# Finer setup loads, halved column maxima and new queue orders in a two-layer decoder kernel

## The chip, the cores and the metric

The kernel runs on one core of one Trainium2 chip. The metric is the device time of one execution in microseconds (us), the median of three runs. The core has a matrix engine (TensorE, PE in the profile, with its weight loads as PEld), a vector engine (VectorE, DVE), an activation engine (ScalarE, ACT), GpSimd (POOL) and a sync engine (SP), which here only issues DMA transfers. All engines run their own instruction streams in order and wait for each other by semaphores.

## The reference

Two decoder layers over 32 sequences of 128 tokens and 256 channels. Each layer is three blocks, each followed by a residual sum and a layer norm:

```
x = LN(x + windowed_attention(x))          # A: 16 heads, window of 7 keys
x = LN(x + cross_attention(x, ctx))        # B: one head, masked
x = LN(x + routed_attention_experts(x))    # X: 8 experts, top 16 tokens each
x = LN(x + decayed_attention(x))           # C: in-block decay mask
x = LN(x + memory_attention(x, ctx))       # D, E: argmax row of ctx, then 16 heads
x = LN(x + bit_ffn(x))                     # F: 256 -> 1024 -> 256

def act_quant(x):      # per token row
    scale = 127 / clip(max(abs(x)), 1e-5)
    return clip(round(x * scale), -128, 127) / scale

def bit_ffn(x):
    h = einsum(act_quant(x), weight_quant(w1))     # 1024 hidden channels
    h = silu(depthwise_conv1d(h, width 3))
    return einsum(act_quant(h), weight_quant(w2))
```

The windowed attention multiplies, for each of seven offsets, the values shifted by -3 to +3 tokens with their weights, and adds the seven products.

## The kernel before

**Tiling.** Two sequences form a group (`GB = 2`, `T = 256` tokens); there are 16 groups. A group goes through nine stations: Q (load of the transposed x, projections to queries, keys and values of the windowed attention), A (the rest of that attention), B, X, C, D, E and F. A tenth, S, is the setup, which runs once. Groups overlap: while one is in F, later ones are in A, B, X and so on.

**Order.** Each engine's instruction stream is written by `walk`, which reads a string of station letters (`ORDER["PE"]`, `ORDER["DVE"]`, `ORDER["ACT"]`, `ORDER["POOL"]`, `ORDER["SP"]`) and each time takes the next step of that station, up to its next `yield`. So an order of some 950 (PE), 1,260 (ACT) and 1,660 (DVE) letters fixes what stands behind what. A step whose semaphore is not there yet holds everything behind it on its engine.

**The start.** SP issues, in this order, the weights `wq0`, `wk0`, `wv0` (256 KB each), the transposed x of group 0 (`xT0`, 256 KB), twelve small and middle loads for the connection weights and constants, the context of group 0 for B, seven factors of products of weights, x of group 0, `xmask` and `wv0x`, the decay bits, and then in one step (line 398 to 402) `wr`, `cos_sin`, `blk`, `iota128`, the expert weights `wqkv_e` (3,072 KB) and `wo_e` (1,024 KB). Only then come the shifts of group 0 (lines 420 to 426): six of the seven windows are copied from SBUF to SBUF by two DMAs each, 252 KB a window. Behind these stand the transposed x of group 1 (line 377), seven loads for D and F (line 404; 801 KB), `raw1` (1,024 KB), x of group 1, the context of group 0 for D (line 438), and `raw2` (1,024 KB). All go through one DMA queue.

On PE, the first step of D (`D0`, key and value projection `wkv1x`) waits for the seven loads of line 404 and for the context of line 438. DVE adds up the shifted windows in thirteen steps (lines 1101 and 1105); PE then turns the sum (line 579), and only then may it project the values of the next group, whose copy by ACT lets SP issue the next shifts. `xT0` and the windows `vw` have one buffer each, so the groups' Q and A form a ring.

**The feed-forward.** The hidden channels come in four pieces of 2 x 128 (`NJ = 4`). For each piece PE multiplies, DVE scales (line 1305), ACT and DVE convolve, gate and take magnitudes, and DVE keeps the running maximum in `top_f`, 128 partitions x 512 (line 1330): columns `i * T + t`, with i the half of the piece and t the token. To get the largest value of each token over all channels, PE turns four blocks of 128 x 128 of `top_f` into `bank_f` (line 889), and DVE reduces 128 x 512 to 128 x 2 (line 1351). The last three setup steps of DVE are the reciprocals of the mean weights and the sum of `w2q` over the hidden channels (line 1039).

Of the kernel before, what the change touches and what calls it, by code (L numbers as in the profile page):

```python
# [11 lines left out]
ALU = mybir.AluOpType  # L12
# [3 lines left out]
P = 128  # L16
# [3 lines left out]
GB = 2  # L20
# [66 lines left out]
        "FEEEEFFEEFFFBBAFFAXXFXBFBFFFAXFAFXAAAAEFEAFXFAAFCCAAAAAAACCFAAFFAXAEEFFQQFFQEQFFFDDDFXXXAXXAXXXXEEXEEFXE"
        "EEEFFFBBFFBAFFABFFFFXXFAAXFFFXAAAEFXAFEAAAFAAAAXAACCEFFFEXCACFFFFEAFAAAQQFFFQDDDAAQXXXXXXXXXFEEXFFFEFEFE"
        "BBEEEAFFXFFBABXXXFFFAAFFXAAEXAFEFFAAAFCCAXFAAAFCFAAAAECEFFXAFFEAAFAQQFFFDDDQAAXXQXXXXXXXEEEXFEXEEEEFFFBF"
        "BFFFAAFFBFBXXXFFAAFFFXAXAAAAEFFCECAAAAACFAAAXFFFCAAXEEAAAFFFFQQEQQFDDDFFFAXXXXXXXAXXEEFXXEFEFFEBFBEEEFFA"  # L90
        "FAFFFBBFXXFXAAFFFXXAAAAAFFEEFCCAAAAFXCFFCAAAAXAEAEFFFFQQQQAEAADDDFXFXXFXXXFXXXAEEAXFEFEEEFFEBEBFXBFFFAAF"
        "FFBXXXFFFFFXEXEAAFFXFAAAACACAAAACFFACFAAAAAAAAEEXFFFFEDDDFQQFQFFXQXEEXXXAAXXXXFEFXEEFEFXBEBEFFFFBAAFFFXX"
        "XFBAAFFFEXXEAFXAAFFAAFAAAAACCAAAAAFFCFCEEAAXAQQQEFFFFAAXQXDDDXXXXFFXXXFFEEEFXEEEEEFFFXBBFFFFAAFXFXBXBFAA"
        "FFFFEEFXXFFAAAAAFAACXCAAAAAACACAFFFEXEAFAAFQQFFEQXXQXXXXFDDDXXXAFAFFXEEEXFEEFFFEEEFBBFFFAAFFFXXFXBBAAFFF"
        "FEEAXAAXAAFFAACCFXAAFCFFCFAEEFFFXAAAEAAAAAFFFDFDDXXAXXXXEEXXXEXFEEEEFEXFFBBFFFFBXXXBFFFFEEXXFFFFFFFCCFXF"
        "FFEECCFFFXEFXXFFXFXXDDDXXXXXXFEEFFFEEFEFEFEFECCFFFFXXFFCXFFCFFXXEEFFFFFEEFFFXDEDXDFFFFEEEFEEEEEFCCFFFFFC"
# [27 lines left out]
class Steps:

# [37 lines left out]
def build(nc, io, out):  # L163
    ctx = ExitStack()
    with ctx:
# [287 lines left out]
        def _(pe):  # L453
# [78 lines left out]
            def queries(g):  # L532
# [3 lines left out]
                if g == 0:  # L536
                    pe.wait_ge(qkv_in, 16 * 3)
# [1274 lines left out]
```

## Time and profile before

| | |
|---|---|
| time, median of 3 runs | 1081.63 us (1080.34 to 1083.15) |
| the profiled execution's own time | 1083.18 us |
| its span, first to last instruction | 1081.4 us |
| PE busy | 938.1 us (87%) |
| weight loads busy | 685.2 us (63%) |
| DVE busy | 864.5 us (80%) |
| ACT busy | 774.6 us (72%) |
| POOL busy | 165.1 us (15%) |
| moved by DMA | 59.04 MB |
| mean granted TensorE clock | 0.957 of full |

Times in the views count from the first instruction. Line numbers are those of the kernel before. In the timeline, consecutive instructions of one kind are merged into one row with their count; the bracket at its end is the idle time of the engine ahead of it and what ended it.

### The profile page before, as it was taken

What the parts mean: (1) busy time and instruction counts of PE and PEld (TensorE: products, weight loads), DVE (VectorE), ACT (ScalarE), POOL (GpSimd) and SP (SyncE); (2) the same over time, 40 slices, a digit from 0 to 9 for tenths busy, and PEclk for the clock granted to TensorE, in tenths of its full rate; (3) what the DMA queues carried; (4) which work ended last, traced back from release to release, by engine and by line L of the source; (5) the groups of instructions that cost most, each with busy time, mean ns of one, the idle gap of its engine ahead of it and who ended that gap; (6) DMA issues with size and microseconds to landing.
All of it is one profiled execution on the core that took longest, in us unless ns stands there. A gap on an engine that the chain in (4) does not pass through costs nothing.

```text
span 1081.4 us, 20184 instructions
## 1 busy us (share of the span) xinstructions
PE 938.1 (87%) x7318; PEld 685.2 (63%) x7318; DVE 864.5 (80%) x2281; ACT 774.6 (72%) x1921; POOL 165.1 (15%) x404
## 2 busy tenths in 40 slices
PE   6588798999998999999999999999999888887652
PEld 4455566767776676767676777777676666565321
DVE  5585775789888979898899989898989785866754
ACT  2166564768877878877788878787878787867653
POOL 2010210202103030302021211212020201010000
PEclk9789999999999999999999999999999999998765
DMA  9723112030120203030302011121102000000000
GB/s 326 237 75 97 38 51 78 1 108 1 42 67 28 70 21 97 11 97 11 98 1 79 30 59 49 36 73 49 59 28 71 11 2 20 2 30 1 11 11 10
DMA packets 36626, 59.04 MB, mean 55 GB/s; under 512 B 6656, under 2 KB 15872, under 8 KB 36016
## 3 DMA queue, kind: packets, MB, share of 16 engines
q1 hardware_dynamic: 36528, 57.76, 17.1%
q8 instruction: 58, 0.95, 0.4%
q14 instruction: 40, 0.33, 0.1%
HBM read 28.77 MB, written 4.19 MB: 30 GB/s over the span
## 4 chain that ended last, share of the span: by engine, by line
PE 55%; ACT 18%; DVE 17%; issue 3%; SPq 2%; DMA 2%; POOL 1%; ACTq 0%; POOLq 0%; DVEq 0%
PE bank_c L456 15%; PE bank_a L456 8%; PE banks_e L456 6%; PE bank_x L456 6%; PE bank_f L456 4%; PE bank_x L666 3%; ACT squares_out L1389 2%; SPq L426 2%; ACT area_e L1605 2%; DVE area_f L1314 2%; DVE neg_top L1254 2%; PE banks_e L835 2%; DMA area_a<-in_xT 2%; ACT area_f L1652 2%; PE bank_a L562 2%
## 5 line engine op out<-in xcount | busy, mean ns | idle before, releaser
L1314 DVE SCALAR_TENSOR_TENSOR area_f<-area_f,w_convw 128x254 f32<-128x254 f32 x256 | 111.7, 478 | 9.2 <-ACT area_f L1639 7.5
L1254 DVE TENSOR_REDUCE neg_top<-banks_e 128x8 f32<-128x1024 f32 x64 | 76.2, 1220 | 30.1 <-PE banks_e L456 29.9
L1377 ACT ACTIVATE area_bx<-bank_x 128x512 f32<-128x512 f32 (+1 forms) x144 | 70.1, 499 | 27.7 <-PE bank_x L666 11.5
L1101 DVE TENSOR_TENSOR area_a<-area_a 128x512 f32<-128x512 f32 x112 | 74.7, 683 | 10.9 <-DMA area_a<-area_a 10.3
L1639 ACT ACTIVATE area_f<-area_f,w_convb,w_convw 128x256 f32<-128x256 f32 x128 | 69.8, 596 | 15.0 <-DVE area_f L1305 14.8
L1046 DVE TENSOR_TENSOR area_a<-area_a 128x512 f32<-128x512 f32 x112 | 73.4, 683 | 5.1 <-PE bank_a L562 2.9
L1605 ACT ACTIVATE area_e<-banks_e 128x512 f32<-128x512 f32 x128 | 68.3, 601 | 8.9 <-PE banks_e L835 8.7
L1377 ACT ACTIVATE area_bx<-bank_c 128x512 f32<-128x512 f32 x64 | 34.3, 536 | 52.9 <-PE bank_c L456 39.4
L1105 DVE TENSOR_TENSOR area_a<-area_a 128x512 f32<-128x512 f32 x96 | 65.8, 685 | 0.3
L1377 ACT ACTIVATE area_a<-bank_a 128x512 f32<-128x512 f32 (+1 forms) x80 | 43.9, 549 | 30.8 <-PE bank_a L456 21.2
L456 PE MATMUL bank_x<-area_bx 128*128 128x128 f32 (+1 forms) x256 | 51.9, 336 | 5.8 <-ACT area_bx L1377 4.3
L456 PE MATMUL bank_a<-area_a,w_wq 128*128 128x256 f32 x128 | 37.1, 442 | 19.1 <-DMA area_a<-in_xT 19.1
L456 PEld LDWEIGHTS bank_x<-area_bx 128*128 128x128 f32 x256 | 40.8, 191 | 17.5 <-ACT area_bx L1377 8.5
L1305 DVE TENSOR_TENSOR area_f<-bank_f,area_f 128x512 f32<-128x512 f32 x64 | 43.8, 684 | 7.7 <-PE bank_f L456 7.7
L456 PE MATMUL bank_f<-area_f,w1q 128*128 128x256 bf16 x256 | 41.8, 290 | 9.3 <-DVE area_f L1305 7.9
L1644 ACT ACTIVATE area_f<-area_f 128x512 f32<-128x512 f32 x64 | 40.4, 632 | 13.0 <-DVE area_f L1314 12.6
L1678 POOL TENSOR_SCALAR bn_negmean_b<-bn_sums_b 128x2 f32<-128x2 f32 x16 | 4.7, 294 | 288.8 <-DVE x L918 288.8
L666 PE MATMUL bank_x<-w_wqkv_e,area_bx 128*32 128x384 f32 x512 | 47.9, 492 | 0.0
L1377 ACT ACTIVATE area_e<-banks_e 128x256 bf16<-128x256 f32 (+1 forms) x64 | 34.5, 540 | 15.6 <-PE banks_e L821 6.8
L1324 DVE SCALAR_TENSOR_TENSOR area_f<-area_f 128x512 f32<-128x512 f32 x64 | 43.8, 684 | 2.1 <-ACT area_f L1644 1.5
L456 PE MATMUL banks_e<-chosen_key,chosen_q 32*128 32x256 f32 x512 | 38.6, 417 | 7.0 <-DVE neg_top L1254 3.9
L1652 ACT ACTIVATE area_f<-area_f 128x512 f16<-128x512 f32 x64 | 37.6, 624 | 9.4 <-DVE area_f L1362 9.4
(315 smaller groups left out, 2635.3 us busy)
## 6 DMA issues: line engine op xcount, KB each, us to landing
area_a<-area_a SPq DMA_DIRECT2D x96, 224.0 KB
area_a<-in_xT SPq DMA_DIRECT2D x16, 256.0 KB, 3.0
area_bx<-in_ctxT SPq DMA_DIRECT2D x16, 256.0 KB, 3.0
x<-in_x SPq DMA_DIRECT2D x16, 256.0 KB, 3.6
area_d<-in_ctxT SPq DMA_DIRECT2D x16, 256.0 KB, 2.9
y<-x SPq DMA_DIRECT2D x16, 256.0 KB, 2.2
w_wqkv_e<-in_wqkv_e SPq DMA_DIRECT2D x1, 3072.0 KB, 11.5
area_f<-in_raw SPq DMA_DIRECT2D x2, 1024.0 KB, 11.1
```

The costliest lines, as they stand in the source:

```text
L456: last = pe.matmul(out_ap, l, r, start=i == 0 and not opened, stop=closes and i == len(pairs) - 1)
L666: last = pe.matmul(bank_x[ES * q:ES * (q + 1), 0:3 * HP], xgf[:, c, e, :], wq[:, c, e, :], start=c == 0, stop=c == DC - 1)
L1046: return dve.tensor_tensor(product_of(wi).rearrange("p (n t) -> p n t", t=P), qT0.rearrange("p c (b t) -> p (c b) t", t=P), kT0.rearrange( ...
L1101: made[wi] = own.mark(dve.tensor_tensor(v4, v4, bc(e4[:, :, wi, :], 3, DH), ALU.mult))
L1105: added = dve.tensor_tensor(vw[:, to, :], vw[:, to, :], vw[:, wi, :], ALU.add)
L1254: dve.tensor_reduce(top[:, b, r:r + 2, :, 0].rearrange("p r (par c) -> p r c par", c=DC), banks_e[:, r:r + 2, :].rearrange("p r (c par k) ...
L1305: dve.tensor_tensor(blocks(th_f[jj % 3], 2), blocks(bank_f[:, :], 2), bc(tscale_f, 1, 2), ALU.mult).then_inc(f_h, 1)
L1314: last = dve.scalar_tensor_tensor(c4[:, i, :, dst], h4[:, i, :, src], cwt3[:, 2 * jj + i, k:k + 1], c4[:, i, :, dst], ALU.mult, ALU.add)
L1377: return act.activation(dst, src, ACT.Copy)
L1605: act.activation(pT_e[:, r * 4 * P:(r + 1) * 4 * P], bank_e[r][:, :], ACT.Exp, scale=float(DH) ** -0.5).then_inc(e_exp, 1)
L1639: last = act.activation(c4[:, i], h4[:, i], ACT.Identity, bias=w["convb"][:, j:j + 1], scale=cwt3[:, j, 1:2])
L1652: act.activation(n2_f[jj], c_f[jj], ACT.Copy, bias=ROUND16).then_inc(f_round, 1)
```

## The change

Four edits.

1. **Setup loads.** `wq0` counts on the semaphore of the transposed x (`xt_in`), `wk0` and `wv0` on their own one, and PE waits for the two only ahead of its second projection. Each of the three is a step of its own; the twelve loads that followed in one step are now two steps of six.
2. **Expert weights.** `wqkv_e` and `wo_e` become steps of their own. In the new SP order they stand behind the shifts of group 0 and the transposed x of group 1.
3. **Column maxima.** DVE takes the maximum of the two halves of `top_f` (128 x 256), PE turns two blocks in place of four, and DVE reduces 128 x 256.
4. **Orders.** All five strings are new. SP's now begins `SSSQSBSASSSSQQSSSASSDAAAABQQ`: after the expert weights come the seven loads of line 404, x of group 1, `raw1`, `raw2`, the context of group 0 for D, x of groups 2 to 5, the context of group 1 for B, the shifts of group 1 and the transposed x of group 2. In DVE's, the sum over `w2q` (line 1039) comes between two window products of group 2, where before it stood amid the window sums of that group. A PE step moves by some two places on average, some by up to sixteen.

```diff
@@ SP @@
             def setup(_):
-                for name in ("wq0", "wk0", "wv0"):
-                    sp.dma_start(w[name][:, :], io[name]).then_inc(qkv_in, 16)
-                yield
+                for name, sem in (("wq0", xt_in), ("wk0", kv_in), ("wv0", kv_in)):
+                    sp.dma_start(w[name][:, :], io[name]).then_inc(sem, 16)
+                    yield
                 for dst, name in ((c1, "c1"), (b1, "b1"), (c2, "c2"), (b2, "b2"), (c3, "c3"), (b3, "b3")):
                     sp.dma_start(dst, io[name]).then_inc(early2_in, 16)
+                yield
                 for name in ("pos", "ident", "headsum", "rows", "part", "wo0"):
...
-                for name in ("cos_sin", "blk", "iota128", "wqkv_e", "wo_e"):
+                for name in ("cos_sin", "blk", "iota128"):
                     sp.dma_start(w[name][:, :], io[name]).then_inc(xw_in, 16)
                 yield
+                for name in ("wqkv_e", "wo_e"):
+                    sp.dma_start(w[name][:, :], io[name]).then_inc(xw_in, 16)
+                    yield
@@ PE @@
             def queries(g):
-                pe.wait_ge(xt_in, 16 * (g + 1))
+                pe.wait_ge(xt_in, 16 * (g + 2))
...
-                if g == 0:
-                    pe.wait_ge(qkv_in, 16 * 3)
                 take("a")
                 project(bank_a, chunked("wq0"), xT0).then_inc(a_qk_proj, 1)
                 until("a", a_qk, 2 * g + 1)
                 yield
+                if g == 0:
+                    pe.wait_ge(kv_in, 16 * 2)
...
                 for b in range(GB):
-                    for i in range(2):
-                        at = (2 * b + i) * P
-                        last = pe.transpose(bank_f[:, at:at + P], top_f[:, i * T + b * P:i * T + (b + 1) * P], I)
+                    last = pe.transpose(bank_f[:, b * P:(b + 1) * P], top_f[:, b * P:(b + 1) * P], I)
@@ DVE @@
-                    last = dve.tensor_tensor(top_f, th_f[jj % 3], top_f, ALU.max)
-                    if jj < NJ - 1:
-                        top_step[0] = own.mark(last)
-                    else:
-                        last.then_inc(f_top, 1)
+                    top_step[0] = own.mark(dve.tensor_tensor(top_f, th_f[jj % 3], top_f, ALU.max))
...
+                dve.wait_ge(own.sem, top_step[0])
+                dve.tensor_tensor(top_f[:, 0:T], top_f[:, 0:T], top_f[:, T:2 * T], ALU.max).then_inc(f_top, 1)
+                yield
                 dve.wait_ge(f_topT, g + 1)
-                m = own.mark(dve.tensor_reduce(am_f, blocks(bank_f[:, :], GB), X, ALU.max))
+                m = own.mark(dve.tensor_reduce(am_f, blocks(bank_f[:, 0:T], GB), X, ALU.max))
@@ ORDER["SP"], first letters @@
-        "SQSBSASSSQQSSADSBQQQQBAAQQBADQQDBAQQBBQDQFAQQDFADBQQFBAFQQADBDQQFBAFAQBQDFBQAQDBQQFADFQDQABDFBAQDDFDFFFF"
+        "SSSQSBSASSSSQQSSSASSDAAAABQQBQQBQQBQQDQDQBDFAQBQDFAQQBDQBQFAFDAQBQFDAQBQDFQBQADFABQQDFABQQDQBFQADFAQBDFD"
```

## Rows read from the trace of the kernel before

**Rows 1.** The page, part 1: busy us, share of the span, instructions

```profile
span 1081.4 us, 20184 instructions
PE 938.1 (87%) x7318; PEld 685.2 (63%) x7318; DVE 864.5 (80%) x2281; ACT 774.6 (72%) x1921; POOL 165.1 (15%) x404
```

**Rows 2.** Windows over long stretches: busy us by engine, PEclk, DMA share, GB/s

```profile
30.00:60.00 30.00, 17.48 (x79) 13.44 (x82) 16.90 (x45) 5.83 (x17) 1.57 (x4) 0.77 0.60 184
60.00:90.00 30.00, 23.31 (x130) 17.15 (x126) 25.78 (x71) 21.58 (x46) 3.84 (x8) 0.89 0.21 62
90.00:120.00 30.00, 22.21 (x154) 15.46 (x147) 21.50 (x44) 15.58 (x38) 3.07 (x4) 0.91 0.29 87
...
240.00:840.00 600.00, 573.42 (x4721) 424.97 (x4713) 540.83 (x1434) 486.31 (x1229) 105.52 (x245) 1.00 0.16 49
...
960.00:1081.00 121.00, 67.10 (x458) 42.36 (x456) 75.37 (x172) 69.74 (x150) 8.33 (x24) 0.74 0.03 9
```

**Rows 3.** Timeline of SP's DMA issues: start us, us, what

```profile
16.82 0.43 SPq L401 DMA_DIRECT2D w_wqkv_e<-in_wqkv_e  x1
...
18.50 8.73 SPq L426 DMA_DIRECT2D area_a<-area_a  x12
27.28 0.53 SPq L377 DMA_DIRECT2D area_a<-in_xT  x1
...
35.63 1.54 SPq L438 DMA_DIRECT2D area_d<-in_ctxT  x1
...
68.03 0.52 SPq L377 DMA_DIRECT2D area_a<-in_xT  x1
```

**Rows 4.** Timeline of DVE around the first window sums

```profile
28.33 0.39 DVE L1090 TENSOR_TENSOR area_a<-area_a 128x224 f32<-128x224 f32 x1
...
39.72 1.89 DVE L1101 TENSOR_TENSOR area_a<-area_a 128x512 f32<-128x512 f32 x3 [10.32 <-DMA area_a<-area_a]
```

**Rows 5.** Timeline of PE, 40 to 71 us

```profile
40.19 3.78 PE L456 MATMUL bank_a<-area_a,w_wq 128*128 128x256 f32 x8 [9.62 <-DMA area_a<-in_xT]
...
55.65 1.15 PE L456 MATMUL bank_c<-w_wkv1x,area_d 128*128 128x144 f32 x8
...
56.78 1.97 PE L456 MATMUL bank_a<-w_wv,area_a 128*128 128x256 f32 x8
...
59.52 1.07 PE L562 MATMUL bank_a<-area_a,w_headsum 128*32 128x256 f32 x16
61.12 0.66 PE L487 MATMUL bank_c<-w_ident,x 128*128 128x128 f32 x4 [0.53 <-ACT x L1396]
...
70.72 3.39 PE L456 MATMUL bank_a<-area_a,w_wq 128*128 128x256 f32 x8 [0.72 <-DMA area_a<-in_xT]
```

**Rows 6.** Windows of 5 us: busy us by engine, PEclk, DMA share, GB/s

```profile
15.00:20.00 5.00, 3.48 (x28) 2.36 (x28) 4.17 (x11) 2.60 (x4) 0.00 (x0) 1.00 1.11 388
...
30.00:35.00 5.00, 0.57 (x3) 0.09 (x2) 0.00 (x0) 0.00 (x0) 0.00 (x0) 0.76 1.05 250
...
60.00:65.00 5.00, 3.40 (x36) 1.89 (x28) 4.56 (x13) 3.55 (x6) 0.00 (x0) 1.00 0.52 158
```

**Rows 7.** Timeline, 112 to 120 us: the sum of w2q, and PE behind it

```profile
112.69 3.64 DVE L1039 TENSOR_REDUCE area_s<-w2q 128x256 f32<-128x2048 f16 x1
...
118.31 1.12 PE L579 MATMUL bank_a<-w_ident,area_a 128*128 128x128 f32 x4 [3.67 <-DVE area_a L1105]
```

**Rows 8.** Timeline of PE at full clock: four turns, two turns

```profile
256.53 0.60 PE L889 MATMUL bank_f<-w_ident,area_f 128*128 128x128 f32 x4
...
256.96 0.39 PE L492 MATMUL bank_c<-w_ident,area_c 128*128 128x128 f32 x2
```

**Rows 9.** Groups of instructions: lines, then a timeline row of the half size

```profile
L1351 DVE TENSOR_REDUCE area_f<-bank_f 128x2 f32<-128x512 f32 x16 | 10.9, 680 | 6.0 <-PE bank_f L889 6.0
...
95.97 0.43 DVE L1193 TENSOR_TENSOR area_bx<-area_bx 128x256 f32<-128x256 f32 x1
...
96.77 0.42 DVE L1123 TENSOR_REDUCE area_bx<-area_bx 128x2 f32<-128x256 f32 x1
```

More of the change, by code:

```diff
@@ L87 @@
[L87 to L96, printed above, removed]
@@ L97 @@
-        "FCFFFFEEFFFFFFFEEFFFDFDDFFFEFEEFFFEEEEEEFFFFFFFFEEFFFFFFFFFFFEEFFFFFFFEFFFFFFFFFFFFFFFFFFFFFFFFFFFFFFF"
+        "SSSQSQQQASSSSASSSASSSSSSSSAASAAASAASSSASSSSAAAAAAAAAAAAQQQQSSSSSSSSSSSSSSAASSSAASSSSSSSSBBSAABSSSSAAABAA"
+        "AAAAAAAAAAAAASSQXXXXXXXXXAXQQQXASAASXBBXXAABAAAXXBXAAAAAAAAAAAAAAAQQQQXAAXXXXXXXXXAXXABBBXBAAXXAAAAAAAAA"
+        "XXAAAXACCAAAAACQQQQXCAAXXXXXXXXXAXXADDDXXEXEAABEEBEEEEXXBAAAAAAAAABAXAAAAEEAAAAQQQCCQCEECXEAAFFFDDDXXXAA"
+        "XXXFXXEXFXEFFXFEEEEEEFBBFFXXBXFFBFAAFFAAAFFFXXFFAAEECCFCXFAAAAAAACAAEEFFFAAAFXFFFEAQQQQFDDDFFFAXXXXXAXXX"
@@ new lines @@
+        "XEXEXFEEEEEFEFFFFBBFFBFFXFAAXXFFBAAEFFAFAAXFXAEAXFAFFCCAAACAAAACEFFFEAQQQFFFFEXQAFAAAFFFDDDAXXXAXXXXXXEF"
+        "EXFXEEEEEFFFBAEBFFFAFBFXXXBFFFFXXAAFEFAAAXEAFAFAACCFAAFCAAAAACEAFFFAAXFFEAQQQQFFEDDDXFXXFFFAXXXXXXAEXEXE"
+        "FEFEEEEFFFBFFFBAAFFBFFFXXXFFAAFBAAAXFXAFXAEEAAAAFFCCAAAAAFCFFCFEEFFXAFQQQEAAFAQXXXXXFFFXDDDXXXAAFFEFEFXF"
+        "AFFEEEEEFEFBBFBAFFFBXXXXAAFAAAFEFXXFFEXAAAFFCCAFAAFFCAAAAAEECFFFXAFAAEAQFQQQFFFXXADDDXXXXXXXAAAEEFXEEEXE"
+        "EEFFFFBBFFXFBFBXXFAFFFAXFAAAFFXAAFFEEAFCCFXAAACAACAAAFFFEEAXAAAFFFFQQQEDDDQFAFFFXXXXXEXEAXXXEFXEXEEEFFFB"
@@ new lines @@
+        "FBFABFFAEFFFXFBXXFFAFFAXAXFAAAAFAFEEFCCAAACAAFFFAAACXAEEAAAQXFFFFQQEQFDDDXXXXXFFFAAXXEEXXFEXEEEFFFEEFXBB"
+        "FFAAFFBFXFBFXXFFFFAAXEXEFFAXFCCFAAAAACFAAACEFFEAAAAAAFAAAXFFFQQQEDDDQXFXFFFXAXXXEEXAXXEFEXEEEFFFEXBBFFFB"
+        "AFAFFXFFBXXFAAFFEAXEXAAFAAXAFFAAAAFFCCFAAAAECAEFFCAAXAFFFFEQQQAQAXXDDDXXFXXXFFFXXAAEXEXEFEEEEEFFFFBBFFFB"
+        "FXXFXBFFFEAAFFEFFXFXAAAAAAAAACCAAAAXFEFCACAFEXFFAAFFFAFQQQEXXXQXXXXDDDXFXFFFAAXXEEEFEEFEEFFEFBBFFFAAFFBF"
+        "XFXXBFFFAAFAAAEAXAAEXFFXACCFFAAAFFFACFFCFEEFAAAAXAAEAFFFFXDDDXXAXXXXXXXXEFEFFEEEEFBBEFEFXBFFXXBFFFFXXFFE"
@@ new lines @@
+        "CXBXCAXCXXBXCQDADXAXDADDDXBXABCEQXEBEEEQEXBCXBCEEXEECECXCEXCADXXDEADEQAXFFDFDDDFABBFFXFBXEBXFFBEEXFEEFCA"
+        "FBCFEFBCXQXFCXEEECEQEXCXDCEFDXFFFEDAXXEFXDFDADDFFAFQBFBXBFFFEXEBFFBXEEEFFCEAFBXACFFBQXCFXEEEECQECXCXEDXF"
+        "FFFCXEDFEDAFXXFFXDADFDDQAFBBXBFFFXEBFFBXEEFEEXFACEBFACBXFFCXQFEEXEECQECXXCCDXDEAXXDFFFFXEEDFDDDAFQFFABFF"
+        "BXBFFFEXFEEFFBEECFXAFCEBFXAFBQXCXBFEEXEECECXQXCFFFEXFDCXXEDXFEDAFFFDFADDDFQAFBFFBFXBXFFBXEBEEEEABCFEAXFC"
+        "BFFXQCXFEEEECEXDXCXCEFFFCXFEQXXDAFEDXFFFADQFDDDABFBXBEFXFFBXBFEEEEFAFEXCFFAFCBQFCXFXQBXCXCEEEEXECDCXDEFF"
@@ new lines @@
+        "FFDAXXEDFEDDDXFAFFQABFFBXBFFFBXBFFFEXFEEEEACFXEBAFCBFXFCXQCXEEXEECQEXCDECXDFFFFXDXEAFXEDFDDDFFAFBFABXBFQ"
+        "FFBXFBEFXEEEEFFACFEXFCBAFXCFBXEECEEQCXECXQDCXDFEXFDFXXFEAXDEFDDDFFFABFABFQBXFFFBXFBEFXFEEEEFAFEXACFBXQFC"
+        "BQFCEEEXECXEXCXECXCDAXXDEFFDFXFEADFQDDDFFFABFFBXBEFFFXBEBEEFXFEFAEBFXFACFBFQCXEEFCEXEXCEXCXCDXCEQXXDXFFF"
+        "DFEAEDFDDDFAFFQABFFBXBFFFBEXFFEEEXBEFFFEACXBACFBFCXFEEXCXEEXDECFFXCFFECBXDEXXEDXFAFFDFADDDFAFXBFBXFBFXBE"
+        "FFEEEEBXCEFFBFXCEFFECFXEEXCXECXFFFCEXDFCXXEDFXEDFFFFDDDDFCXCFFCFXFFCXFCEFFFEEEEXCFEDXFXCEEXEEXFEFDXFFDEX"
@@ L112 @@
+        "DEXDDDFECFFFCFCFECEFFFECEEFFCFEFFDCFEEEEFDEFDEFFDFFDDEDFEFFFFEFEEEEFFFEFFFEEFFEEFFEFEFFFFEFEFFFFFFFFFFFF"
         "FFFFFFFFFF"
```

45 lines of the change are left out of this document (16 added, 29 removed).

## The prediction

> **What bounds the kernel now.** I read the page's busy times first [rows 1]: PE has 938.1 us of work in a span of 1081.4 us, so it stands idle for 143.3 us, and DVE for 217. The average hides three different stretches, so the second view is the table of long windows [rows 2]. From 240 to 840 us PE is busy 573.42 of 600 us (96%) at full clock, DVE 540.83 (90%): there the length is PE's work plus 4% of gaps, and whatever reaches PE earlier at 240 us ends the stretch earlier by as much. From 30 to 60, 60 to 90 and 90 to 120 us PE does 17.48, 23.31 and 22.21 us of work, so 27 us are idle within 90, with the clock at 0.77, 0.89 and 0.91 of full. The last 121 us hold 67.10 us of PE work: one or two groups, a chain of latencies.
>
> So the start is where time can be had. The third view is SP's issues [rows 3] beside the waits of DVE and PE [rows 4, 5]. The shifts of group 0 are issued from 18.50 us to 27.23, the transposed x of group 1 at 27.28. DVE has its weights at 28.72 and is through its other steps at 29.40 (39.72 less 10.32 of idling), and yet adds the first window at 39.72, when the shifts have landed [rows 4]. PE waits 9.62 us for the transposed x, until 40.19 [rows 5]. What they wait for is the traffic ahead of them in the one queue: 4,096 KB of expert weights, issued at 16.82 us [rows 3]. The 5-us windows say that the transfer engines are full then: share 1.11 and 388 GB/s at 15 to 20 us, 1.05 and 250 GB/s (shifts among them) at 30 to 35 us [rows 6]. At 388 GB/s 4,096 KB (4.19 MB) take 10.8 us, which is the wait.
>
> **The change part by part.**
>
> *Weights behind the shifts.* SP reaches the shifts no sooner, since they wait for ACT's copy of the values. Without the 4.19 MB ahead they should land as those of a later group do: the transposed x issued at 68.03 lets PE start at 70.72 [rows 3, 5], 2.7 us later. From 27.28 that gives 30.0 us for both, DVE gains 39.72 - 30.0 = 9.7 us and PE 10.2. PE's projection also finds a warm clock: eight matmuls took 3.78 us after the long idle and 1.97 us later [rows 5], worth some 1.8 us. In the new order DVE adds its thirteen windows almost without setup steps between (about 0.6 us each, the three of 39.72 take 1.89), so they end near 38.5. PE turns them, and projects the values of group 1 near 42, where it ended at 58.75 before.
>
> That lead isn't kept whole. Behind the values PE has the output projection of group 0, the first head sums of group 1, and then the first step of D, and it waits for loads that now stand behind the weights: weights 4,096 KB, the seven loads 801, x 256, raw1 and raw2 2,048, context 256, together 7,457 KB or 7.64 MB. From 27.8 us at 388 GB/s that is 19.7 us, with 2.7 us until they are seen 50.2 us. Behind that step stand the second scores of A, the chain of B and all the rest, so PE idles from about 46 to 50. It did that step at 55.65 before, and then the values (1.97) and the first head sums (1.07) of group 1 [rows 5], which now lie ahead of it. So the lead behind it is 55.65 - 50.2 + 3.0 = 8.5 us. The next point is the transposed x of group 2: x of groups 2 to 5 and a context (1,280 KB, 3.4 us) also stand ahead, then the shifts (5 us at share 0.52 over 8.7 us [rows 3, 6]); it is there near 59.5. PE reaches it 70.72 - 61.12 = 9.6 us after the turning of x for B [rows 5], which starts near 52.5, so near 62: 8.7 us ahead. I take 9 us. The ends: at the 250 GB/s of the worst window the 7.64 MB take 30.6 us, D's step comes at 61.1, 5.5 us later than before, less 3.0: a loss of 2.5 us. With no hindrance the lead is the 10.2 us and the 1.8 of clock: 12 us. The window with 250 GB/s is one in which shifts moved, the loads here are from HBM, so I stay near the 388.
>
> The Trainium skill, page "DMA: Bandwidth & Descriptors", section Specifications, gives a core some 358 GB/s from HBM. By that the 7.64 MB take 21.3 us, D's step comes at 51.8, and the lead would be 1.6 us smaller; the trace goes beyond that figure with 388 GB/s in the window from 15 us.
>
> *Finer steps for wq0, wk0, wv0, and the waits.* Nothing: the transposed x is issued fourth in both orders and lands last. The context of B now stands ahead of six small loads: DVE's first setup step comes up to 1 us later (256 KB at 250 to 388 GB/s), and DVE has that slack, since it was free 0.6 us ahead of the new landing of the shifts and its products wait for ACT. 0 us, at worst -1.
>
> *The sum of w2q.* It takes 3.64 us on DVE amid the window sums of group 2, and PE behind it idles for 3.67 us and then works at half clock: four turns in 1.12 us [rows 7] where 0.60 is the full-clock time [rows 8]. In the new order it stands between the products of group 2, ahead of the second head sums. Some of it falls into DVE's own waits there, some delays the products. Between 0 and 5 us (idle, and some 1.4 of clock); I take 2.5.
>
> *Column maxima.* On PE four turns take 0.60 us and two take 0.39 [rows 8]: 0.21 us less, 16 times, 3.4 us. In the stretch in which PE is busy 96% this shortens the group's period; in the first and last groups it doesn't count as such, so 3.0 us, between 0 and 3.4. On DVE the reduction falls from 680 ns to 420, and a 128x256 maximum of 430 ns is added [rows 9]: +0.17 us a group at most, 2.7 us in all. DVE is 90% busy next to PE's 96 [rows 2], so it is covered by 59 us of DVE idle in that stretch; in the last group it is on the path: 0.43 - 0.26 - 0.21 = 0 us. Uncovered it would cost 2.7 us.
>
> The Trainium skill, page "Trainium Kernel Development and Optimization", section Performance Expectations, warns that matmul busy time is a poor measure, since matmuls are pipelined, and sends one to the weight loads; these are busy 424.97 of 600 us, 71% [rows 2]. By that PE needn't be the bound in the middle, and the 3.0 us of this term would be nothing.
>
> *The orders.* A PE step moves by some two places. What they can move is the idle time: 26.6 us in the middle stretch [rows 2], some 2.5 us a group. I see no step that must win or lose, and take 0, with 6 us to either side, which is half a microsecond a group.
>
> **Sum.** 9 + 2.5 + 3.0 + 0 = 14.5 us. The profiled execution took 1083.18 us for a span of 1081.4; that gives 1066.9 for the span and 1068.7 for its time. The median of the runs shown is 1081.63, 1.55 below the profiled one, so I forecast **1067 us**, 1.3% faster. A difference of 0.3%, 3.2 us, is about what a measurement here can tell from none.
>
> **The rivals.**
>
> *The loads take the shifts' place.* PE stands in the queue at D's first step until far beyond 50 us. For it: 7.64 MB in a row, and rates of 250 GB/s occur. Against it: before, the share of the transfer engines over 30 to 60 us was 0.60 [rows 2], which is 18 us of full traffic, so nearly the same bytes were through by about 48. With a lead of 0 in place of 9 and the rest as above, 1076 us: faster still, by 0.5%; with the loss of 2.5 and half of the rest, 1081.
>
> *PE waits at the column maxima, slower.* The place is PE's turning of `top_f` in each group. It now needs one more DVE step behind the last maximum, and DVE's order puts up to two score steps of C between. If PE comes there too early by the new step (0.43), two score steps (0.42 each) and the wait for the step ahead, 1.3 us a group, 16 groups cost 20.8 us: 1081.6 - 14.5 + 20.8 = 1088 us. It decides from 0.9 us a group. For it: DVE is 90% busy and in order. Against it: before, DVE also had other steps between the last maximum and the reduction, and PE can be given other work ahead of the turns.
>
> *No change.* The start's gain is spent in the middle, because another station's ring (the single banks, one buffer each) sets the period and the earlier start only makes groups wait. Then only clock and 1 or 2 us remain: 1080 us. Against it speaks PE's 96%.
>
> *More.* Lead 12, all 5 us of the sum, 3.4, and the new orders save 5: 25 us, 1056.
>
> **Chances.** Forecast case (1060 to 1074, likeliest 1067) 0.57; more (below 1060) 0.08; lead lost (1074 to 1081) 0.16, of which 0.10 faster than 1078.4; no change (1078.4 to 1084.9) 0.08; slower (1088) 0.11. So faster by over 0.3%: 0.57 + 0.08 + 0.10 = 0.75; within 0.3%: 0.06 + 0.08 = 0.14; slower 0.11. The range from 1056 to 1081 leaves out 0.04 below and some 0.15 above. The forecast case alone has 1060 to 1074.
>
> **What would show it.** Right: DVE's first window sum and the projection of group 1 near 30 us, with waits for DMA below 2 us; D's first step near 50 us with a DMA wait of some 4 us; the transposed x of group 2 used near 62 us; PE idle of under 19 us from 30 to 120 us, not 27; no 3.6-us gap of PE behind the windows of group 2; PE's busy time lower by 3 to 6 us; 240 to 840 us still 95 to 96% full. Wrong: D's step beyond 55 us, PE waits named by the maximum's line in the middle, or a middle stretch at 94%, which at 16 groups costs 12 us and takes nearly all back.

## The result, and the profile after

The changed kernel takes 1052.78 us (median of 4 runs, 1049.99 to 1054.87) where the kernel before, run beside it, takes 1082.39 us: ratio 0.9723, interval 0.969 to 0.9756. That is 29.6 us, twice the 14.5 us forecast, and 3.2 us below the lower end of the range. The profiled execution took 1053.05 us. The page of the changed kernel, part 1:

```profile
span 1051.3 us, 20136 instructions
PE 931.0 (89%) x7286; PEld 676.7 (64%) x7286; DVE 869.9 (83%) x2297; ACT 776.9 (74%) x1921; POOL 161.3 (15%) x404
```

Against [rows 1] PE has 7.1 us less work and 23.0 us less idle time (120.3 in place of 143.3). So three quarters of the gain is idle time that went. The long windows of the changed kernel say where:

```profile
30.00:60.00 30.00, 20.34 (x110) 15.31 (x110) 23.93 (x66) 10.44 (x25) 2.51 (x4) 0.87 1.01 362
60.00:90.00 30.00, 26.20 (x162) 18.23 (x160) 26.77 (x64) 23.87 (x50) 4.18 (x8) 0.90 0.19 57
90.00:120.00 30.00, 26.79 (x174) 20.69 (x178) 22.33 (x60) 16.73 (x45) 4.80 (x12) 1.00 0.21 63
...
240.00:840.00 600.00, 576.09 (x4691) 427.54 (x4690) 544.39 (x1459) 489.40 (x1234) 107.37 (x260) 1.00 0.16 49
```

Beside [rows 2], PE does 73.33 us of work between 30 and 120 us, not 63.00; the middle stretch holds 2.67 us more. The start went as forecast, step by step. SP's issues of the changed kernel, beside [rows 3]:

```profile
17.98 10.01 SPq L431 DMA_DIRECT2D area_a<-area_a  x12
28.04 0.53 SPq L378 DMA_DIRECT2D area_a<-in_xT  x1
28.62 0.42 SPq L406 DMA_DIRECT2D w_wqkv_e<-in_wqkv_e  x1
...
39.86 0.45 SPq L443 DMA_DIRECT2D area_d<-in_ctxT  x1
...
47.43 8.58 SPq L431 DMA_DIRECT2D area_a<-area_a  x12
56.05 0.53 SPq L378 DMA_DIRECT2D area_a<-in_xT  x1
```

and its steps of DVE and PE, beside [rows 4, 5]:

```profile
29.74 0.68 DVE L1104 TENSOR_TENSOR area_a<-area_a 128x512 f32<-128x512 f32 x1
...
30.86 1.99 PE L461 MATMUL bank_a<-area_a,w_wq 128*128 128x256 f32 x8 [1.12 <-DMA area_a<-in_xT]
...
50.60 2.26 PE L461 MATMUL bank_c<-w_wkv1x,area_d 128*128 128x144 f32 x8 [3.28 <-issue]
...
62.63 3.50 PE L461 MATMUL bank_a<-area_a,w_wq 128*128 128x256 f32 x8
```

The first window sum is at 29.74 us, not 39.72; the projection of group 1 at 30.86, not 40.19; D's first step at 50.60 (forecast 50.2), behind a wait that the trace puts down to "issue" and that ends when the loads are in (the context of D, issued at 39.86 us, landed 10.7 us later); the projection of group 2 at 62.63 (forecast 62), 8.1 us ahead of [rows 5]. The sum over `w2q` now starts at 81.4 us, the window sums of group 2 at 95.38, and the turns of that group come with no gap in front of them:

```profile
81.42 3.77 DVE L1042 TENSOR_REDUCE area_s<-w2q 128x256 f32<-128x2048 f16 x1
...
95.38 1.90 DVE L1104 TENSOR_TENSOR area_a<-area_a 128x512 f32<-128x512 f32 x3
...
103.52 0.66 PE L584 MATMUL bank_a<-w_ident,area_a 128*128 128x128 f32 x4
```

They stood at 118.31 behind 3.67 us of idling [rows 7]. So the lead is 8 us at 62 us and 15 us at 104. It doesn't stop there. A mark that comes once a group and late in it is PE's row on `w_sums,offset`, at the end of each group's feed-forward. Its rows of groups 0, 8 and 15 in the kernel before:

```profile
272.28 0.38 PE L899 MATMUL bank_f<-w_sums,offset 128*128 128x512 f16 x1
...
739.02 0.39 PE L899 MATMUL bank_f<-w_sums,offset 128*128 128x512 f16 x1
...
1070.64 0.61 PE L899 MATMUL bank_f<-w_sums,offset 128*128 128x512 f16 x1 [3.24 <-ACT area_f L1652]
```

Those of groups 0 and 15 in the changed kernel:

```profile
253.06 0.38 PE L902 MATMUL bank_f<-w_sums,offset 128*128 128x512 f16 x1
...
1040.10 0.61 PE L902 MATMUL bank_f<-w_sums,offset 128*128 128x512 f16 x1 [3.24 <-ACT area_f L1654]
```

The difference is the lead of a run at that output. I call the outputs F0 to F15, by group, and use their leads below; this table has the kernels that split the change. Each figure is the time of the row in the kernel before less that in the run, in us, from one profiled execution each; "ratio" is of times, from 4 to 12 executions of the kernel and 4 to 29 of the kernel before.

| kernel | F0 | F4 | F9 | F12 | F15 | ratio to before, interval |
|---|---|---|---|---|---|---|
| changed kernel | 19.2 | 20.3 | 20.6 | 25.9 | 30.5 | 0.9723 (0.969 to 0.9756) |
| new loads only | 6.0 | 6.0 | 5.7 | 6.9 | 11.4 | 0.993 (0.9908 to 0.9953) |
| new loads, D's step later | 11.0 | 11.0 | 10.5 | 11.7 | 8.8 | 0.9911 (0.988 to 0.9941) |
| all new to 125 us, then old orders | 14.2 | 13.7 | 13.3 | 14.6 | 17.0 | 0.9875 (0.9853 to 0.9897) |
| all old to 125 us, then new orders | 4.7 | 5.8 | 6.1 | 11.5 | 18.2 | 0.9862 (0.9838 to 0.9885) |
| changed, weights ahead again | 10.6 | 11.8 | 12.1 | 17.5 | 24.9 | 0.9787 (0.9755 to 0.982) |
| new orders from F8 on only | -1.2 | -1.3 | -3.5 | 1.1 | 7.1 | 0.993 (0.9903 to 0.9957) |
| halved maxima only | -1.5 | -2.0 | -2.4 | -1.1 | 0.7 | 1.0008 (0.9988 to 1.0029) |
| changed, four turns | 20.1 | 21.7 | 21.2 | 25.9 | 33.0 | 0.9722 (0.9692 to 0.9752) |

Within one order of the queues the distance between two outputs up to F9 repeats to under a microsecond (F0 to F9 is 521.7 us in the kernel before, 522.0 with the new loads). Ahead of F0 and behind F12 it doesn't: eight runs whose code is that of the kernel before up to 125 us have leads from -2.7 to 2.2 us at the shifts of group 3, and eight whose code is the same from 260 us on (bar one context load) gain from -2.9 to 4.5 us between F12 and F15. There the ratio decides.

### The profile page after: what moved, and what is told of

Same layout as the page of the kernel before. It is cut to its first block, busy times and chain, and to the rows that moved or that the text cites. A ratio compares the mean times of both kernels' runs of the same rounds, so it can differ in the third digit from the quotient of the medians.

```text
span 1051.3 us, 20136 instructions
## 1 busy us (share of the span) xinstructions
PE 931.0 (89%) x7286; PEld 676.7 (64%) x7286; DVE 869.9 (83%) x2297; ACT 776.9 (74%) x1921; POOL 161.3 (15%) x404
## 3 DMA queue, kind: packets, MB, share of 16 engines
q1 hardware_dynamic: 36528, 57.76, 17.5%
## 4 chain that ended last, share of the span: by engine, by line
PE 53%; DVE 20%; ACT 19%; issue 4%; POOL 2%; SPq 1%; DMA 1%; ACTq 0%; POOLq 0%; DVEq 0%
PE bank_c L461 16%; PE bank_a L461 8%; PE banks_e L461 7%; PE bank_x L461 5%; PE bank_f L461 3%; DVE neg_top L1257 3%; ACT squares_out L1391 3%; DVE area_f L1317 3%; PE bank_x L671 3%; ACT area_e L1607 2%; PE banks_e L840 2%; PE bank_a L567 2%; DVE x L921 2%; ACT area_f L1641 2%; ACT area_bx L1379 2%
## 5 line engine op out<-in xcount | busy, mean ns | idle before, releaser
L1257 DVE TENSOR_REDUCE neg_top<-banks_e 128x8 f32<-128x1024 f32 x64 | 76.6, 1219 | 17.5 <-PE banks_e L461 17.4
L1379 ACT ACTIVATE area_a<-bank_a 128x512 f32<-128x512 f32 (+1 forms) x80 | 44.1, 551 | 24.3 <-PE bank_a L461 20.8
L1379 ACT ACTIVATE area_e<-banks_e 128x256 bf16<-128x256 f32 (+1 forms) x64 | 34.7, 542 | 13.3 <-PE banks_e L492 5.8
L461 PE MATMUL banks_e<-area_e,chosen_v 128*32 128x512 f32 x256 | 35.9, 633 | 8.7 <-ACT area_e L1607 8.3
## 6 DMA issues: line engine op xcount, KB each, us to landing
w_wqkv_e<-in_wqkv_e SPq DMA_DIRECT2D x1, 3072.0 KB, 10.7
```

The lines of the kernel that those rows point to most:

```text
L461: last = pe.matmul(out_ap, l, r, start=i == 0 and not opened, stop=closes and i == len(pairs) - 1)
L1257: dve.tensor_reduce(top[:, b, r:r + 2, :, 0].rearrange("p r (par c) -> p r c par", c=DC), banks_e[:, r:r + 2, :].rearrange("p r (c par k) ...
L1379: return act.activation(dst, src, ACT.Copy)
```

## The experiments

In the short diffs a step is written as its station, its group and a name (`A1.heads1` is the first head sums of group 1 in station A, `D0.kv` the projection of keys and values in D); "..." stands for steps left out.

### The change taken apart

*New loads only*: the kernel before with edits 1 and 2, its orders otherwise kept.

```diff
 SP: ... wr..iota
-    wqkv_e wo_e  shifts 0  xT 1 ...
+    shifts 0  xT 1  wqkv_e wo_e ...
```

> The kernel before with the new loads alone: the expert weights behind the shifts of group 0 and the transposed x of group 1, wq0, wk0 and wv0 as single steps; all other orders and the column maxima as before. Theory 1 (the loads cost the wait at 30 to 40 us, and the rest of the 29.6 us is the orders'): the first window sum and the projection of group 1 start near 30 us, but PE's old order has the first step of D ahead of the values of group 1, so it waits there for the context behind 7.6 MB, until about 50 us; a lead of 6 to 10 us, 1072 to 1076 us. Rival (the weights were all of the start's loss and the orders add nothing there): a lead of 16 us, near 1066 us.

Measured: 1075.38 us, ratio 0.993, a lead of 6.0 to 6.1 us from the shifts of group 3 to F7. In this run PE has D's step ahead of the values of group 1, as before:

```profile
47.27 2.26 PE L460 MATMUL bank_c<-w_wkv1x,area_d 128*128 128x144 f32 x8 [4.52 <-issue]
49.32 3.15 PE L460 MATMUL bank_a<-w_wv,area_a 128*128 128x256 f32 x8
```

*Halved maxima only*: the kernel before with edit 3 and one more DVE step a group.

```diff
 DVE: ... F.third maximum
+    F.maximum of the halves
```

> The kernel before with the halved column maxima alone: one more DVE step straight behind the last maximum of each group, two turns in place of four. Theory 1 (PE is the bound in the middle, so its 3.4 us less of work count): 1079 us, 2.5 to 3.5 us faster. Rival (matmul busy time isn't the bound, or the DVE step costs as much as it saves): 1081 to 1083 us.

Measured: 1084.68 us, ratio 1.0008 (0.9988 to 1.0029). Its middle stretch:

```profile
240.00:840.00 600.00, 570.28 (x4681) 422.08 (x4679) 540.71 (x1438) 485.54 (x1227) 104.95 (x244) 1.00 0.16 49
```

PE's work there fell by 3.14 us [rows 2], and its idle time rose by the same.

*Changed, four turns*: the counter-test, edit 3 undone in the new orders.

> The changed kernel with the column maxima as before: four turns, a reduction of 128x512, no DVE step for the halves; all orders otherwise those of the change. Theory 1 (the turns that fall away are worth nothing, since the group's period is a chain through several engines and not PE's sum of work): within 1.5 us of the changed kernel, 1051 to 1055 us. Rival (the new orders were laid for the shorter work and only there it counts): 3 us slower, 1056 us.

Measured: 1052.72 us, ratio 0.9722 beside 0.9723. Two ratios with intervals of 0.3% to either side couldn't tell 3 us from none. The leads can: from F0 to F9, nine groups, the halved maxima gave 0.3 us in the new orders and cost 0.9 in the old ones, where 0.21 us a group would be 1.9. Both are within the scatter of that distance, so the forecast term is out in either order.

*Changed, weights ahead*: edit 2's place undone in the new orders.

```diff
 SP: ... wr..iota
+    wqkv_e wo_e
     shifts 0  xT 1
-    wqkv_e wo_e
```

> The changed kernel with the expert weights put back ahead of the shifts of group 0; all else as changed. Theory 1: the first window sum starts near 40 us again, D's first step finds its loads, and the new orders of the start keep some 6 us; 1059 to 1063 us. Rival (under the new orders the place of the weights is worth no more than the 6 us that it is worth under the old): 1059 us; rival 2 (all 14 us of the start are the weights' place): 1067 us.

Measured: 1060.03 us, ratio 0.9787: the place of the weights is worth 7 us here, and by the leads 8.6 at F0.

*All new to 125 us* and *all old to 125 us*: the four changed queues cut where both orders have done the same letters (PE behind 87 steps, ACT 104, DVE 222, SP behind the transposed x of group 4). The first has the new loads and start, the second the old ones; both have the halved maxima. POOL's two orders are alike in their first 22 steps; its queue is the old one in the first run and the new one in the second.

> New loads, new column maxima, and the new orders only up to the fourth group's projections (87 steps of PE, 104 of ACT, 222 of DVE, SP up to the transposed x of group 4), then the old orders to the end. Theory 1: 16 us of the start and 3.4 us of turns, 1061 to 1063 us, 9 to 11 us slower than the changed kernel. Rival (all of the gain beyond the turns is made at the start, and the later idle time falls by itself once the start is early): within 2 us of the changed kernel, 1053 to 1055 us.

> Old loads and old orders up to the fourth group's projections, then the new orders, with the new column maxima throughout. Theory 1: 3.4 us of turns and 10 us of idle time, 1067 to 1070 us. Rival (the later orders are worth nothing by themselves): 1078 us.

Measured: 1070.03 us (0.9875) and 1068.48 us (0.9862), 13.5 and 14.9 us; together 28.4 of the 30. So the change has two halves of one size, and the second holds nothing but orders, beside the maxima.

### The sum over w2q

The kernel before, with this one step moved behind the last window sum of group 2.

```diff
 DVE: window sums of group 2, amid them
-    sum over w2q
      ... last window sum of group 2
+    sum over w2q
```

> The kernel before with one DVE step moved: the sum of w2q behind the window sums of group 2 in place of amid them. Theory 1: PE's idle 3.7 us at 114.6 us and the half clock behind it fall away, but the sum now delays the products of group 3: 2 to 5 us faster, 1079 to 1082 us beside 1084. Rival (it only moves the delay on): no difference.

Measured: 1083.92 us, ratio 1.0001 (0.9977 to 1.0026). The sum now began at 115.2 us, behind all window sums, and the 3.67-us gap became two, ahead of the turns and behind them:

```profile
117.14 0.63 PE L579 MATMUL bank_a<-w_ident,area_a 128*128 128x128 f32 x4 [1.91 <-ACT area_a L1377]
...
124.90 0.33 PE L487 MATMUL bank_c<-w_ident,x 128*128 128x128 f32 x1 [2.81 <-ACT x L1396]
```

This is a later place than that in the changed kernel, which has the sum ahead of the window sums. The sum alone at that earlier place wasn't run.

### D's first step

*D's loads first*: in the changed kernel the seven loads and D's context stand ahead of the expert weights.

```diff
 SP: xT 1
-    wqkv_e wo_e  seven loads  x 1  raw1 raw2  D ctx 0
+    seven loads  D ctx 0  wqkv_e wo_e  x 1  raw1 raw2
```

> The changed kernel with the seven loads for D and F, and the context of group 0 for D, ahead of the expert weights. Theory 1: PE's first step of D no longer waits at 47 to 50.6 us (3.3 us) and the clock doesn't fall behind it (four rows of matmuls then took 3.5 us too long in all); the lead grows by 3 to 6 us if the transposed x of group 2 is there in time, 1047 to 1050 us. Rival (the transposed x of group 2 and the shifts of group 1, queued behind the same bytes, set the end of this stretch): 1052 to 1053 us, no change.

Measured: 1052.85 us, ratio 0.9706 (0.9674 to 0.9738), not to be told from the changed kernel's. D's step no longer waits, and the wait stands at the transposed x of group 2:

```profile
47.66 1.25 PE L461 MATMUL bank_c<-w_wkv1x,area_d 128*128 128x144 f32 x8
...
63.77 2.50 PE L461 MATMUL bank_a<-area_a,w_wq 128*128 128x256 f32 x5 [3.55 <-DMA area_a<-in_xT]
```

*New loads, D's step later*: *new loads only* with one step moved.

```diff
 PE:  A0.wo
-     D0.kv
      Q1.v  S.t_b  A1.heads1
+     D0.kv
 ACT: B0.v
-     D0.kv
      A0.sq  Q1.v  ...  A0.nm
+     D0.kv
```

> The run with the new loads and old orders, and one step moved: the first keys and values of the experts (TensorE's D step, which waited 4.52 us at 45 us for data, with its ScalarE eviction) stands behind the third projection of group 1 and the first heads of group 1, as in the changed kernel. Theory (new loads and new start orders together gave 14 us where the loads gave 6, and most of the 8 is this one move, since the second shifts no longer wait behind the D step): the second group's shifts are issued 12 to 13 us earlier than in the kernel before, 6 more than with the loads alone; the feed-forward outputs are 9 to 13 us ahead; time 1070 to 1074, ratio 0.988 to 0.992. Rival (the 8 us came from the other moves between 60 and 120 us, where TensorE's last wait for VectorE of 3.67 us went): the shifts come earlier but the lead at the first feed-forward output stays at 6 to 7 us, ratio 0.9925 to 0.994.

Measured: 1073.08 us, ratio 0.9911, leads of 11.0 us from F0 to F6. The values of group 1 no longer stand behind the wait:

```profile
43.84 1.97 PE L460 MATMUL bank_a<-w_wv,area_a 128*128 128x256 f32 x8 [0.96 <-DVE x L922]
...
47.58 1.25 PE L460 MATMUL bank_c<-w_wkv1x,area_d 128*128 128x144 f32 x8
```

With them the shifts of group 1 go out at 46.47 us, not 53.12, and DVE has its windows earlier. In these two profiled executions the moved step is worth 5 us of lead; by the two ratios it is 2 us, which the intervals don't tell from none, and executions of equal code lie up to 4.9 us apart there. So the earlier shifts are shown, and the size isn't.

*Changed, D's step later still*, behind the second heads of group 1.

```diff
 PE:  A1.heads1
-     D0.kv
      S.t_b  A1.heads2
+     D0.kv
```

> The changed kernel with the experts' first step one place later still, behind the second heads of group 1, so that TensorE does not stand 3.28 us before it at 47 to 50 us. Theory (the wait is filled by 1.93 us of heads, and the rest of the start follows): 1 to 2.5 us faster than the changed kernel, ratio 0.970 to 0.9715. Rival (TensorE then waits for VectorE's products of the second heads at about the same place, or the second group's shifts set the pace anyway): no lead over the changed kernel at the second group's shifts, ratio 0.972 to 0.973.

Measured: 1052.22 us, ratio 0.9715 (0.9689 to 0.9741). Its profile is 1.6 us ahead of the changed kernel's from F0 to F12, the wait is at VectorE's numbers:

```profile
48.78 0.38 PE L461 MATMUL bank_f<-area_s,onesb 128*128 128x1 f32 x2 [1.48 <-DVE area_s L1018]
49.10 1.06 PE L567 MATMUL bank_a<-area_a,w_headsum 128*32 128x256 f32 x12
50.09 1.25 PE L461 MATMUL bank_c<-w_wkv1x,area_d 128*128 128x144 f32 x8
```

By its time it can't be told from the changed kernel, and start times of equal code differ by as much.

*The version to which these point*: four turns, and D's step there.

> The changed kernel with four turns for the column maxima, as before, and the experts' first step behind the second heads of group 1. Each alone could not be told from the changed kernel by its time (ratios 0.9722 and 0.9715 beside 0.9723), though the latter was 1.6 us ahead of it in the profile from the third shifts on. Theory (the two are independent, and the halved maxima cost VectorE what they save TensorE): 1050 to 1052 us, ratio 0.9695 to 0.9715. Rival (neither is worth anything): ratio 0.972 to 0.973.

Measured: 1053.29 us, ratio 0.9719 (0.9698 to 0.9739), leads of 18.9 at F0 and 20.4 at F4. So the rival holds: none of these versions beats the changed kernel by a difference that its time shows.

### The later orders

*New orders from F8 on*: cut behind 679 steps of PE (ACT 867, DVE 1205, POOL 66, SP behind the shifts of group 14), the rest the kernel before.

> The kernel before, with the changed kernel's orders only from the ninth feed-forward output on (about 739 us to the end). From the run with new orders at the start alone and the one with new orders from group 4 on I read 5 to 7 us of gain between the tenth feed-forward output and the end. Theory (the changed orders shorten the stretch in which the scans and turns run out): the time falls by 5 to 8 us, ratio 0.9925 to 0.9955, with the lead opening between the tenth and the fourteenth feed-forward output, and none before. Rival A (that gain came from feed-forwards that stood earlier in the order already, so a late start of the new order buys under 2 us): ratio 0.998 to 1.001. Rival B (it came from TensorE's granted clock in the last 100 us, which differs from one execution to the next): the lead follows the clock of that stretch and not the order, ratio within 0.3% of 1.

Measured: 1076.32 us, ratio 0.993 (0.9903 to 0.9957): 7.6 us. In the profile it falls back by 2 us from F8 to F9, grows by 4.6 to F12 and by 6.0 more to F15. The windows of the kernel before and then of this run, PE's work alone:

```profile
900.00:950.00 50.00, 42.82 (x364) 0.97 0.04 12
950.00:1000.00 50.00, 38.28 (x287) 0.92 0.05 16
1000.00:1040.00 40.00, 25.32 (x188) 0.76 0.02 8
```

```profile
900.00:950.00 50.00, 43.42 (x371) 1.00 0.04 12
950.00:1000.00 50.00, 38.33 (x320) 0.97 0.04 12
1000.00:1040.00 40.00, 23.79 (x155) 0.67 0.04 14
```

PE is as busy from 950 to 1000 us, but gets through 320 instructions, not 287, at a clock of 0.97, not 0.92. Part of the lead may thus be clock, and the run doesn't say whether the order brings the clock or the execution does. But not all of it is: the eleven executions of this run had mean granted clocks of 0.956 to 0.963, and seven executions of the kernel before taken beside them had the same. Their median is 1081.52 us, 5.2 us above this run's 1076.32.

*New orders in the middle*: between 125 and 170 us for PE, ACT and DVE; then SP's queue alone; then both; then all of them up to about 260 us. In SP's queue the experts' context loads of groups 1 and 2 move behind the shifts:

```diff
 SP: xT 4  B ctx 3  x 4
-    D ctx 1
     shifts 4  xT 5
-    D ctx 2
+    D ctx 1
     B ctx 4  x 5  shifts 5
+    D ctx 2
```

> The kernel before with four turns and old loads; only the orders of one stretch are the changed kernel's: TensorE's steps 88 to 132, ScalarE's 105 to 157, VectorE's 223 to 299 (about 125 to 170 us). The run that had the new orders from there to the end was 5.1 us ahead by the fifth group's shifts and 4.7 ahead at the first feed-forward output. Theory (the gain of that stretch lies in the order of these steps alone): the output of the first feed-forward comes 4 to 5.5 us earlier, nothing is gained or lost behind it, and the time is ratio 0.995 to 0.9965, some 1078 to 1079. Rival A (the old orders behind it are laid out for the old times and give the lead back): ahead by 4 to 5 at the fifth shifts, under 2 at the second feed-forward output, ratio 0.998 to 1.001. Rival B (the gain needs the new orders behind as well): no lead at the fifth shifts.

> The kernel before with one change, in SyncE's queue alone: the loads of the experts' context for groups 1 and 2 stand behind the fifth and the sixth shifts, not ahead of them. In the kernel before the first of them was issued at 170.62 us and the fifth shifts right behind it at 171.00, although TensorE had the third projection of that group done at 163.45. Theory (the shifts were held in the queue by the context load, which waits for its buffer): the fifth shifts are issued at about 164 to 165 us (6 to 7 earlier), and the first feed-forward output comes 3 to 5 us earlier; ratio 0.995 to 0.9975. Rival A (the old orders of the compute engines do not use earlier shifts): the shifts come 6 earlier and the feed-forward outputs under 1 us; ratio 0.9985 to 1.001. Rival B (the experts' context then comes too late and TensorE waits for it, 2 us or more): ratio 1.001 to 1.003.

> The run with TensorE's, ScalarE's and VectorE's new orders between 125 and 170 us, which gained nothing, with the same change of SyncE's queue besides. Theory (both are needed: the queue frees the shifts, the compute orders use them): the fifth shifts are issued 5 to 7 us earlier than in the kernel before, the first feed-forward output 4 to 5; ratio 0.995 to 0.997. Rival (the queue alone does it): the same as the queue's change alone, within 1 us at the feed-forward outputs. Rival B (neither, the gain needs the new orders behind it): under 1 us.

> The kernel before with four turns and old loads, and the changed kernel's orders from about 125 to 260 us in the queues of TensorE (steps 88 to 206), ScalarE, VectorE and SyncE (to the shifts of group 6); old orders ahead and behind. Theory (the gain of the middle needs the shifts brought forward and all orders up to the first feed-forward output, and is then kept): the lead that stood at the fourth shifts grows by 4 to 5 us by the first feed-forward output and stays to the end within 1 us, ratio 0.995 to 0.997. Rival (it is given back as soon as the old orders go on, as the queue's 6.8 us were): lead under 2 us at the second feed-forward output, ratio 0.998 to 1.001.

SP's rows of the kernel before, and of the run with the queue alone:

```profile
170.62 0.33 SPq L438 DMA_DIRECT2D area_d<-in_ctxT  x1
171.00 9.89 SPq L426 DMA_DIRECT2D area_a<-area_a  x12
```

```profile
165.66 8.59 SPq L426 DMA_DIRECT2D area_a<-area_a  x12
...
174.88 0.42 SPq L438 DMA_DIRECT2D area_d<-in_ctxT  x1
```

The shifts of group 4 were indeed held by a load that waited for its buffer. But freeing them showed no gain in time:

| kernel | lead at shifts 3 | shifts 4 | shifts 5 | F0 | F4 | ratio, interval |
|---|---|---|---|---|---|---|
| compute orders to 170 us | 2.2 | 1.8 | 2.7 | 2.7 | 2.7 | 1.0035 (1.001 to 1.006) |
| SP's queue alone | -1.5 | 5.3 | -0.7 | -1.6 | -1.6 | 1.0008 (0.9982 to 1.0033) |
| both | 1.8 | 6.9 | 4.1 | 3.2 | 3.2 | 0.9992 (0.9964 to 1.002) |
| all to 260 us | -2.7 | 2.4 | 1.8 | 1.1 | -1.0 | 0.999 (0.9969 to 1.001) |
| all to the end (second half) | 0.6 | 5.7 | 5.1 | 4.7 | 5.8 | 0.9862 (0.9838 to 0.9885) |

With the queue alone the 6.8 us at the fourth shifts are gone a group later. The more of the orders behind are new, the more is kept, but with all of them to 260 us the gain at F0 (3.8 over the third shifts) is down to 1.8 at F1, where the old orders run again. My theories for these four runs failed, and so did each rival that put the gain into one place; the rivals by which the old orders don't use the lead, or give it back, are the ones that held.

*Last context load behind the last shifts*, SP's queue alone in the kernel before.

```diff
 SP: y of group 9
-    B ctx 15
     x 15  shifts 15
+    B ctx 15
```

> The kernel before with one change, in SyncE's queue alone: the context load of the last group stands behind the last shifts. It was issued at 809.13 us and the last shifts at 813.91, after TensorE's last third projection; so it was not what held them there. Theory (the 7 to 8 us of the end come from the compute engines' orders, not from this queue): last shifts within 0.5 us, ratio within 0.2% of 1. Rival (the queue holds them, as I suppose for the fifth): last shifts 3 to 6 us earlier, ratio 0.994 to 0.997.

Measured: 1083.85 us, ratio 1.001 (0.9987 to 1.0033), the lead at the last shifts is that at the shifts of group 14, ahead of the edit (-2.4 us both). The 7.6 us of the end aren't in this queue.

## Why the prediction was wrong

**Weights behind the shifts: 9 us, right.** Every time forecast was met within 1 us (30.0, 50.2, 62). With D's step behind the values and heads of group 1, as my sum had it, the loads give 9.6 us by the ratio and a lead of 11.0; alone they give 7.6 and 6.0; with the weights put back the changed kernel lost 7 and 8.6. The "+ 3.0" of my sum, for the values and heads that go ahead of D's step, came out as 2 us by the ratios and 5 by the leads; the step also brings the shifts of group 1 forward by 6.65 us, which I hadn't counted. By the rate in the Trainium skill, "DMA: Bandwidth & Descriptors", Specifications (some 358 GB/s a core from HBM), D's step would have come at 51.8 us; it came at 50.60, between the two forecasts, and the changed kernel's 5-us windows from 30 to 50 us hold 424, 408, 400 and 393 GB/s, so the trace stays above the page's figure throughout.

**The sum over w2q: 2.5 us, not settled.** Moved alone to a later place it is worth 0: the wait for DVE became two for ACT. At the place that the change gives it, it wasn't moved alone. There the window sums of group 2 take 8.0 us from first to last (95.38 to 103.34), where with the sum amid them they took 11.6 (106.60 to 118.17), and in all seven profiles with the new start orders the lead grows by 7.3 to 7.6 us between the transposed x of group 3 and the shifts of that group. So the gap did close as forecast. But with the old orders behind, 3.0 of these us are lost again at the next shifts. The start as a whole came out near its terms: 9 + 2.5 forecast, 13.5 us measured by the ratio; of its lead of 14.2 at F0, 11.0 is there with loads and D's step alone, and some 3 are the other moves ahead of 125 us, the sum among them, which I haven't taken apart.

**Column maxima: 3.0 us, wrong.** By the ratios they measured 0 in both orders, by the leads 0.3 us and a loss of 0.9. From [rows 2] I read that "there the length is PE's work plus 4% of gaps". The work did fall by 3.14 us in the middle stretch, and the idle time rose by it. My reading is that the 4% of gaps hold a loop through several engines, of which PE's turns are only a part, and that DVE got a step more in that loop; which loop it is no run shows. The rival in which PE loses 20.8 us there didn't occur either: with the halved maxima alone PE waits for them once between 240 and 840 us, 0.3 us. The Trainium skill, "Trainium Kernel Development and Optimization", Performance Expectations, warns against matmul busy time as a measure; by that the term was 0, and the runs agree with the result. They don't show that weight loads are what counts in its place: these are busy 71% here.

**Orders: 0 us, at most 6, the step that failed.** "I see no step that must win or lose, and take 0, with 6 us to either side, which is half a microsecond a group." Measured: 14.9 us for the orders behind 125 us alone, and some 3 more in the start beyond D's step, which my sum had in its first term. The error was in the shape: I spread the unknown evenly over groups, and bounded it by the idle time of the middle stretch (26.6 us). But the middle gives 1.4 us from F0 to F9. The rest lies at the two ends, where the idle time is: some 4.7 us up to F0 (0.6 of it at the shifts of group 3, where equal code scatters), and behind F8 the 7.6 us that the new orders give there alone. [Rows 2] had it: PE works 67.10 of the last 121 us, and I named that stretch a chain of latencies and left it out of the sum.

**What stays open.** The 7.6 us of the end have been put to a stretch, not to a step; at like clocks 5.2 of them are left. The 4 to 5 us between the fourth group and F0 exist only with the new orders behind them; no part of these orders gave them alone. What the sum over `w2q` is worth at its new place is open. Why the compute orders by themselves were 0.35% slower, though their profiled execution isn't, is open too.

## What to carry to other kernels

In a kernel whose engines run fixed orders, an engine that is 96% busy isn't yet the bound: take the work away in one run and see whether the idle time grows by it. Then look for what an order can give at the ends, where the stations fill and drain, and price it from the idle time there, not from the middle. Moving one transfer past a blocked one shifts its time by the full wait and may change nothing; what counts is the order of everything that is to use it.

## What the hardware showed unexpectedly

D's step took 2.26 us behind the 3.28-us wait and 1.25 us where there was none, and the eight matmuls of a projection 3.15 to 3.78 us behind waits of 4.5 and 9.6 us and 1.97 where PE had worked on: the long waits of the start are paid a second time. The windows of the changed kernel, PE's work, its granted clock and what the transfers moved, around the wait for D's data:

```profile
40.00:45.00 5.00, 3.98 (x17) 1.00 1.08 400
45.00:50.00 5.00, 1.07 (x16) 0.88 1.01 393
50.00:55.00 5.00, 4.40 (x23) 0.50 1.08 309
55.00:60.00 5.00, 2.76 (x18) 0.84 0.91 236
60.00:65.00 5.00, 4.53 (x12) 0.50 0.03 8
```

PE worked 1.07 of 5 us, and the clock of the next five was the lower level, 1.2 GHz where 2.4 is full. The 3.28 us of waiting cost 1.0 us more in D's step alone. It fell once more behind shorter gaps: from 55 to 60 us PE worked 2.76 of 5 us, the next five were at the lower level again, and the projection of group 2 at 62.63 took 3.50 us with no wait listed ahead of it.

The end is where equal code differs most. With the same orders from 125 us to the end, the distance from F12 to F15 was 117.8 us in the kernel before, 113.2 with the new loads and 120.7 with the new loads and D's step later, while F0 to F9 agreed within 0.5 us.
